# Spreading softmax reciprocals through DRAM instead of TensorE transposes, with a new order on every engine

## The chip, the cores and the metric

The kernel runs on one core of a Trainium2 chip. Its time is the device time of one execution in microseconds. Three runs of the kernel before took 716.42, 717.45 and 717.95 us; the median is 717.45 us. One further execution was profiled.

## The reference

`x` is (32, 256, 384) in float32: 32 batches of 256 nodes with 384 features. `adj` is (32, 256, 256) and is added to the attention scores. For every batch:

```python
q = x @ Wq.T;  k = x @ Wk.T;  v = x @ Wv.T + bv        # 12 heads of 32
a = einsum('bnhd,bmhd->bhnm', q, k) * 384**-0.5 + adj   # one adj for all heads
a = where(all(a == 0, axis=-1), -inf, a)
a = nan_to_num(softmax(a, axis=-1))
o = einsum('bhnm,bmhd->bnhd', a, v).reshape(B, N, 384) @ Wo.T + bo
out = layernorm(x + o)                                   # over the 384 features
```

The kernel leaves the softmax unnormalised (exponentials, and their sums per head and row), multiplies the exponentials with v, and divides the result, `o`, by the sums. The part of this case is that division. `o` stands in the bank with (head, dimension) on the partitions and the 256 rows on the free axis, while the sums stand with the rows on the partitions and (half, head) on the free axis. So the reciprocal of a sum has to be turned, and repeated over the 32 dimensions of its head, before it can be multiplied.

## The kernel before, in words

Each of the five engines runs a list of instructions of its own, and the lists meet in semaphores. The order in each list is written out by hand: `start()` for the first batches, `step(t)` for a general batch, `end()` for the last ones. There is no planner at run time: an engine that meets a wait stands still, with all that is behind it. The unit of repetition is a batch t. While TensorE is at the scores of batch t, the division and the output projection belong to batches t-1 and t-2 (`prev`, `prev2` in the code), and the first projections to t+1 and t+2 (`nxt`, `nxt2`).

What is done for a batch:

- TensorE (`block.tensor`). Every projection is done as three products of split numbers (high by high, high by low, low by high), all through line 787: `project_kq` three times (K01, Q12 into `bank_c`, K2Q0 into `bank_b`), `project_v` twice and `project_y` twice (`bank_b`). `scores` (line 836) is done for three groups of four heads. `transposes` (line 847) turns four of the twelve units of exponentials into `bank_t`; the other eight are turned by VectorE and two DMAs. `weigh` (line 877) multiplies exponentials with v, one group of four heads at a time, always into the same half of `bank_a`. `flag` (line 884) is a small product that finds out whether any row's maximum is zero. `spread` (line 858) is the step that the change removes: `spread(t, 0)` transposes `inv_wide` four times into `bank_c`, `spread(t, 1)` twice into `bank_t`.
- ScalarE. `exps` (line 559): 24 exponentials of 128x256 with their sums. `save_kq` (lines 538, 542), `copy_probT` (line 569), `save_o` (line 576, which copies the weighed bank to `o_raw`, three times), `split_o_hi` (line 584), `normalise` (line 590).
- VectorE. `add_bias` (line 1192, 24 instructions of 128x256, each with a read of its accumulator), `square` (line 1209, eight 32x32-block transposes of 128x512), `save_v` (line 1229), `find_zero` (line 1235), `read_flag` (line 1240), `mask` (a register load and a branch that is hardly ever taken into its body), `invert` (line 1264, the reciprocal of the 24 sums), `divide` (line 1273, in two parts: 128x512 out of `o_raw` and `bank_c`, 128x256 out of `o_raw` and `bank_t`), `residual` (line 1292), `moments` (lines 1297 and 1302).
- GpSimd. Splits of x, of k and q and of `o`, `permute_bias`, `add_bo`, `deviation`, and `widen_inv` (line 418), which repeats each reciprocal 32 times along the free axis for `spread`.
- SyncE issues all DMAs, in one queue (q1). `store_squares` (line 248) and `load_squares` (line 257) move a group of turned exponentials to DRAM and back, twice a batch; `load_xt`, `load_bias`, `load_xr` and `store_out` move inputs and output. SyncE too waits in its order.

The chain of the reciprocals before: `invert` (VectorE), `widen_inv` (GpSimd), `spread` (TensorE), `divide` (VectorE). The weighed bank is freed by `save_o` on ScalarE, and TensorE waits for `o_saved[g]` before it weighs the next group or runs `flag`, whose result lies in the same bank.

Of the kernel before, what the change touches and what calls it, by code (L numbers as in the profile page):

```python
# [3 lines left out]
F32 = mybir.dt.float32  # L4
# [8 lines left out]
H, HD = 12, 32  # L13
# [67 lines left out]
def build(nc, x, xT, adj, wqT, wkT, wvT, bv, woT, bo, out):  # L81
    def sb(name, shape, dt=F32):
# [23 lines left out]
    sums = [sb(f"sums{p}", [P, NT, H]) for p in range(2)]  # L106
# [15 lines left out]
    most = sb("most", [P, NT, H])  # L122
    inv = sb("inv", [P, NT, H])
    inv_wide = sb("inv_wide", [P, NT, H, HD])
    o_raw = [sb(f"o_raw{p}", [P, KC, N]) for p in range(2)]
    o_n = sb("o_n", [P, KC, N])
# [19 lines left out]
    bank = {"R0": bank_c, "K01": bank_c, "Q12": bank_c, "PV0": bank_a, "PV1": bank_a, "PV2": bank_a,  # L146
            "K2Q0": bank_b, "V0": bank_b, "V1": bank_b, "Y0": bank_b, "Y1": bank_b}
    t_flat = bank_t[:].rearrange("p k m q -> p (k m q)")
    bank["R1"] = t_flat
# [4 lines left out]
    last_bank = {"R0": s_flat[0], "Y0": s_flat[0], "R1": s_flat[1], "Y1": s_flat[1], "PV1": s_flat[2], "PV2": bank_c[:]}  # L154
# [42 lines left out]
    o_saved = [sem(f"o_saved{g}") for g in range(KC)]  # L197
# [4 lines left out]
    inv_wide_ready = sem("inv_wide_ready")  # L202
    inv_spread = sem("inv_spread")
# [11 lines left out]
    CONSTS = 4  # L215
# [7 lines left out]
    with nc.Block() as block:  # L223

        @block.sync
        def _(sp):
# [32 lines left out]

            def store_out(t):  # L260
# [27 lines left out]
            def start():  # L288
# [5 lines left out]
                load_bias(t1)  # L294
                load_xt(t2)
                load_xr(t0)
                store_squares(t0, 0)
                load_xr(t1)
                load_squares(t0, 0)
                load_xt(t3)  # L300
                store_squares(t0, 1)
                load_xt(t4)
                load_squares(t0, 1)
                load_bias(t2)
                store_squares(t1, 0)
                store_squares(t1, 1)
                load_squares(t1, 0)
                load_squares(t1, 1)
                load_bias(t3)
                store_squares(t2, 0)  # L310
                load_squares(t2, 0)
                load_xr(t2)
                store_squares(t2, 1)
                load_bias(t4)
                load_squares(t2, 1)
                store_squares(t3, 0)
                store_out(t0)

            def step(t):
                nxt2 = t.later(2)  # L320
                nxt = t.later(1)
                prev2 = t.later(-2)
                load_xt(nxt2)
                load_bias(nxt2)
                load_squares(t, 0)
                store_squares(t, 1)
                load_squares(t, 1)
                load_xr(t)
                store_squares(nxt, 0)
                store_out(prev2)  # L330

            def end():
                t28 = Batch(28)
                t29 = Batch(29)
                t30 = Batch(30)
                t31 = Batch(31)
                store_squares(t30, 1)
                load_squares(t30, 0)
                load_squares(t30, 1)
                store_squares(t31, 0)  # L340
                load_xr(t30)
                load_squares(t31, 0)
                store_squares(t31, 1)
                store_out(t28)
                load_squares(t31, 1)
                store_out(t29)
                load_xr(t31)
                store_out(t30)
                store_out(t31)

            start()
            for c in range(3, 30):
                step(Batch(c))
# [4 lines left out]
        def _(pool):  # L358
# [3 lines left out]
            pool.wait_ge(const_ready, 3)  # L362
# [41 lines left out]
            def split_o_lo(t, k):  # L404
# [5 lines left out]
                nc.gpsimd.tensor_tensor(o_lo[:, a:b], o_n[:, a:b], o_hi[:, a:b].bitcast(F32), ALU.subtract  # L410
                                        ).then_inc(o_ready, 1)
# [1143 lines left out]
```

## Time and profile before

| | |
|---|---|
| median of three runs | 717.45 us (716.42 to 717.95) |
| the profiled execution | 718.51 us |
| its span, first to last instruction | 716.2 us |
| mean granted TensorE clock | 0.997 |
| TensorE busy with matmuls | 698.7 us |
| VectorE / ScalarE / GpSimd busy | 600.1 / 613.8 / 487.2 us |
| queue q1, share of 16 DMA engines | 72.3% |

The span is 2.3 us shorter than the execution's own time; the rest lies around the first and the last instruction. A matmul's duration in the trace runs from its start to its modelled end, and the next one starts long before that end. So the time that a block of matmuls takes of TensorE is read from its start to the start of the next block. The same holds, less strongly, for VectorE and ScalarE.

### The profile page before, as it was taken

The page shows a single profiled execution, that of the slowest core. Times are in us where ns is not written, and L with a number is a line of the kernel's source. Part 1 is how long each engine was busy: PE and PEld are TensorE (multiplying, and loading weights), DVE is VectorE, ACT ScalarE, POOL GpSimd, SP SyncE. Part 2 cuts the span into 40 slices and gives each one's busy share as a digit, 9 for nine tenths or more (in the row PEclk, how much of TensorE's full clock was granted, in tenths as well). Part 3 has the DMA queues.
Part 4 walks back from the last instruction along what each step waited for, and adds up shares of the span by engine and source line. Part 5 has one row for each costly group of instructions (what it writes and reads, how often), then busy time and mean ns, then how long its engine had stood idle before and what let it go on. Part 6 is the DMA issues. An engine that isn't in the chain of part 4 may idle for free.

```text
span 716.2 us, 23143 instructions
## 1 busy us (share of the span) xinstructions
PE 698.7 (98%) x7557; PEld 600.7 (84%) x7557; DVE 600.1 (84%) x2220; ACT 613.8 (86%) x1993; POOL 487.2 (68%) x548
## 2 busy tenths in 40 slices
PE   8999999999999999999999999999999999999895
PEld 8878888888888888888888888888898888888774
DVE  4898988889888889888889888889888889888973
ACT  4889988889988889988888988889888888898882
POOL 4767666677766678766677766678766677766452
PEclk9999999999999999999999999999999999999998
DMA  8475877787777687777787777787777777777672
GB/s 266 152 278 206 300 267 264 252 315 236 263 263 273 241 309 240 265 264 267 251 302 240 262 267 259 252 305 247 257 270 261 262 291 248 255 273 259 248 288 90
DMA packets 84008, 184.61 MB, mean 258 GB/s; under 512 B 4272, under 2 KB 42928, under 8 KB 75696
## 3 DMA queue, kind: packets, MB, share of 16 engines
q1 hardware_dynamic: 83888, 183.12, 72.3%
q8 instruction: 61, 1.00, 0.6%
q14 instruction: 59, 0.48, 0.2%
HBM read 103.42 MB, written 79.69 MB: 256 GB/s over the span
## 4 chain that ended last, share of the span: by engine, by line
PE 85%; DVE 5%; DMA 4%; issue 2%; POOL 2%; ACT 1%; SPq 0%; DVEq 0%; ACTq 0%; POOLq 0%
PE bank_b L787 34%; PE bank_c L787 16%; PE bank_a L877 12%; PE s_bank L836 11%; PE bank_t L847 8%; PE bank_c L858 2%; DVE neg L1192 2%; DMA sq_dram<-w_f 2%; DMA sq_probT<-sq_dram 2%; ACT prob L559 1%; PE bank_t L858 1%; DVE w_f L1209 1%; DMA xt<-in_xT 1%; POOL kq_lo L400 0%; DVE y L1292 0%
## 5 line engine op out<-in xcount | busy, mean ns | idle before, releaser
L559 ACT ACTIVATE prob<-neg,negmax 128x256 f32<-128x256 f32 x768 | 380.3, 500 | 51.8 <-DVE w_f L1209 34.3
L1192 DVE CUSTOM_DVE_ANT_0 neg<-s_bank,bias_sq 128x256 f32<-128x256 f32 x512 | 185.2, 414 | 49.0 <-issue 42.6
L1209 DVE STREAM_TRANSPOSE w_f<-prob 128x512 f32<-128x512 f32 x256 | 173.2, 696 | 0.7 <-ACT prob L559 0.7
L559 ACT ACTIVATION_READ_ACCUMULATOR prob<-neg,negmax 128x1 f32 x768 | 147.7, 192 | 0.0
L400 POOL TENSOR_TENSOR kq_lo<-kq,kq_hi 128x512 fp32r<-128x512 f32 x96 | 125.2, 1304 | 7.7
L398 POOL CAST kq_hi<-kq 128x512 fp32r<-128x512 f32 x96 | 60.2, 627 | 79.3 <-issue 73.9
L787 PE MATMUL bank_c<-xt_hi,w_hi 128*128 128x256 f32 x384 | 111.1, 289 | 1.0 <-DVE w_lo L1171 1.0
L787 PE MATMUL bank_c<-xt_hi,w_lo 128*128 128x256 f32 x384 | 108.3, 282 | 0.0
L787 PE MATMUL bank_c<-xt_lo,w_hi 128*128 128x256 f32 x384 | 108.3, 282 | 0.0
L1192 DVE CUSTOM_DVE_ANT_0 neg<-s_bank,bias 128x256 f32<-128x256 f32 x256 | 91.0, 420 | 15.2 <-PE s_bank L836 15.0
L847 PE MATMUL bank_t<-ident,prob 128*128 128x128 f32 x512 | 80.3, 279 | 0.7 <-ACT probT L569 0.7
L569 ACT ACTIVATE probT<-bank_t 128x512 f32<-128x512 f32 x128 | 75.0, 586 | 3.6 <-PE bank_t L847 2.9
L787 PEld LDWEIGHTS bank_c<-xt_hi,w_hi 128*128 128x128 f32 x384 | 73.0, 190 | 2.1 <-issue 1.7
L410 POOL TENSOR_TENSOR o_lo<-o_n,o_hi 128x512 fp32r<-128x512 f32 (+1 forms) x62 | 63.4, 1025 | 15.4 <-ACT o_hi L584 15.4
L787 PEld LDWEIGHTS bank_c<-xt_hi,w_lo 128*128 128x128 f32 x384 | 73.1, 190 | 0.0
L787 PEld LDWEIGHTS bank_c<-xt_lo,w_hi 128*128 128x128 f32 x384 | 73.1, 190 | 0.0
L877 PE MATMUL bank_a<-sq_probT,v 128*32 128x256 f32 x1008 | 67.5, 385 | 1.2 <-DVE zero_flag L1240 1.0
L787 PE MATMUL bank_b<-w_hi,o_hi 128*128 128x384 f32 x186 | 68.3, 367 | 0.3 <-DVE y L1292 0.3
L787 PE MATMUL bank_b<-w_hi,xt_hi 128*128 128x384 f32 x192 | 67.8, 353 | 0.3 <-ACT kq L542 0.2
L836 PE MATMUL s_bank<-kq_hi 32*128 32x256 f32 x768 | 65.2, 328 | 2.6 <-POOL kq_lo L400 1.3
L836 PEld LDWEIGHTS s_bank<-kq_hi 32*128 32x128 f32 x768 | 37.3, 183 | 34.4 <-issue 33.3
L847 PEld LDWEIGHTS bank_t<-ident,prob 128*128 128x128 f32 x512 | 56.5, 140 | 10.7 <-issue 1.6
(88 smaller groups left out, 1794.1 us busy)
## 6 DMA issues: line engine op xcount, KB each, us to landing
sq_dram<-w_f SPq DMA_DIRECT2D x64, 1024.0 KB, 4.5
sq_probT<-sq_dram SPq DMA_DIRECT2D x64, 1024.0 KB, 5.6
xt<-in_xT SPq DMA_DIRECT2D x32, 384.0 KB, 4.5
xr<-in_x SPq DMA_DIRECT2D x32, 384.0 KB, 6.2
out_y<-y_out SPq DMA_DIRECT2D x31, 384.0 KB, 3.0
bias<-in_adj SPq DMA_DIRECT2D x32, 256.0 KB, 3.2
w_f<-in_wkT SPq DMA_DIRECT2D x3, 192.0 KB, 4.5
w_f<-in_wqT SPq DMA_DIRECT2D x3, 192.0 KB, 5.0
```

Of the source, the lines that this page charges most:

```text
L398: nc.gpsimd.tensor_copy(kq_hi[t.p][:, a:a + 2, :], kq[:, a:a + 2, :]).then_inc(kq_hi_ready[name], 1)
L400: nc.gpsimd.tensor_tensor(kq_lo[t.p][:, a:a + 2, :], kq[:, a:a + 2, :], kq_hi[t.p][:, a:a + 2, :].bitcast(F32), ALU.subtract).then_inc(kq_ ...
L410: nc.gpsimd.tensor_tensor(o_lo[:, a:b], o_n[:, a:b], o_hi[:, a:b].bitcast(F32), ALU.subtract).then_inc(o_ready, 1)
L559: nc.scalar.activation(prob[:, u % PROB_RING, k], neg[:, h, w.c], ACT.Exp, scale=-1.0, bias=negmax[t.p][:, w.c, h:h + 1], accum_out=sums[t ...
L569: nc.scalar.activation(probT[:, a:a + PAIR, :, P * w.c:P * (w.c + 1)], bank_t[:], ACT.Copy).then_inc(probT_act, 1)
L787: last = nc.tensor.matmul(ps, w_pair[a](k), m_pair[b](k), start=(k == 0 and e == 0), stop=(k == KC - 1 and e == 2))
L836: last = nc.tensor.matmul(s_bank[j][:, c, :], a[t.p][rows, KC + g, P * c:P * (c + 1)], b[t.p][rows, g, :], start=(e == 0), stop=(e == 2))
L847: last = nc.tensor.transpose(bank_t[:, k, m, :], prob[:, u % PROB_RING, k, P * m:P * (m + 1)], ident[:])
L858: last = nc.tensor.transpose(bank_at(t, f"R{k}")[:, at:at + P], inv_wide[:, c, JH * g:JH * (g + 1), :].rearrange("p h d -> p (h d)"), iden ...
L877: last = nc.tensor.matmul(bank_at(t, f"PV{g}")[HD * j:HD * (j + 1), 0:N], v[t.p][:, m, HD * h:HD * (h + 1)], weights, start=(m == 0), stop ...
L1192: nc.vector.tensor_tensor_reduce(out=neg[:, h, w.c], in0=s_bank[h % JH][:, w.c, :], in1=by[t.p][:, w.c, :], scale=-1.0, scalar=BIG, op0=AL ...
L1209: nc.vector.transpose(sq_stage[w.g][:, :, a:a + PAIR, :, w.c].rearrange("p b h m s -> p (h m) b s"), prob[:, u % PROB_RING].rearrange("p k ...
```

## The change

- `spread` and `widen_inv` go, and with them `inv_wide` and the banks R0 and R1. `save_o` and `o_raw` go too.
- The sums are laid out as (head in group, group, half), 24 columns. `invert` writes their reciprocals into a 128x32 tile whose last 8 columns stay at 1.0 (a new memset at the start).
- `turn_inv`, new on VectorE, waits for `invert` and transposes the 128x32 tile in 32x32 blocks.
- `store_inv`, new on SyncE, stores the turned tile to DRAM (16 KB). Four `load_inv` read it back, one for each head in group j: 768 numbers, given to 32 partitions each, into `inv_all` (128 x 3 x 256; two buffers).
- `divide` is done three times a batch, once for each group g, and reads the weighed bank itself and `inv_all`. TensorE now waits for `o_n_ready` where it waited for `o_saved`. `o_n` gets a second buffer.
- `load_xt` runs three batches ahead instead of two, `store_out` three behind instead of two, `save_kq` K01 and `project_kq` K01 two ahead instead of one.
- The order of the list of every engine is new; `step` runs over batches 3 to 28 instead of 3 to 29, and `end` covers 29 to 31.

```diff
+            def store_inv(t):
+                sp.wait_ge(inv_turned, t.count(1, 1))
+                apart(sp)
+
+                after(sp, inv_loaded[t.p], JH * (t.loads() - DMA))
+                sp.dma_start(inv_dram[t.p].rearrange("k b r -> b k r"),
+                             inv_t[:]).then_inc(inv_stored[t.p], DMA)
+
+            def load_inv(t, j):
+
+                sp.wait_ge(inv_stored[t.p], t.loads())
+                apart(sp)
+
+                after(sp, o_n_ready, t.count(KC, -KC))
+                row = inv_dram[t.p][KC * NT * j:KC * NT * (j + 1)].rearrange("k b r -> (k b r)")
+                sp.dma_start(inv_all[t.p][HD * j:HD * (j + 1)].rearrange("p g n -> p (g n)"),
+                             row.rearrange("(a n) -> a n", a=1).to_broadcast([HD, KC * N])
+                             ).then_inc(inv_loaded[t.p], DMA)
...
             def step(t):
+                nxt3 = t.later(3)
                 nxt2 = t.later(2)
                 nxt = t.later(1)
-                prev2 = t.later(-2)
-                load_xt(nxt2)
+                prev3 = t.later(-3)
                 load_bias(nxt2)
+                load_xt(nxt3)
+                store_squares(t, 1)
                 load_squares(t, 0)
-                store_squares(t, 1)
+                store_out(prev3)
+                store_inv(t)
                 load_squares(t, 1)
+                load_inv(t, 3)
+                load_inv(t, 0)
+                load_inv(t, 2)
+                load_inv(t, 1)
                 load_xr(t)
                 store_squares(nxt, 0)
-                store_out(prev2)
...
-            def widen_inv(t):
-                pool.wait_ge(inv_ready, t.count(1, 1))
-
-                after(pool, inv_spread, t.count(2))
-                apart(pool)
-                nc.gpsimd.tensor_copy(inv_wide[:], inv[:].unsqueeze(3).to_broadcast([P, NT, H, HD])
-                                      ).then_inc(inv_wide_ready, 1)
...
+            def turn_inv(t):
+                dve.wait_ge(inv_ready, t.count(1, 1))
+
+                if t.c >= 1:
+                    dve.wait_ge(inv_stored[1 - t.p], t.later(-1).loads())
+                apart(dve)
+                nc.vector.transpose(inv_t[:], inv[:]).then_inc(inv_turned, 1)
+
+            def divide(t, g):
+                dve.wait_ge(pv_done[g], t.count(1, 1))
+                if g == 0:
+                    dve.wait_ge(inv_loaded[t.p], JH * t.loads())
+
+                    after(dve, o_ready, t.count(2, -2))
+                    apart(dve)
+                nc.vector.tensor_tensor(o_n[t.p][:, g, :], bank_at(t, f"PV{g}")[:, 0:N], inv_all[t.p][:, g, :],
                                         ALU.mult).then_inc(o_n_ready, 1)
```

The new step of VectorE and of TensorE, in order:

```
VectorE: invert(t-1), turn_inv(t-1), divide(t-2,2), add_bias(t,4..7), square(t,0), save_v(t,1),
         square(t,1..3), add_bias(t,8..10), square(t,4), add_bias(t,11), divide(t-1,0), find_zero(t),
         square(t,5..7), read_flag(t), residual(t-2,0), mask(t), divide(t-1,1), add_bias(t+1,0..1),
         residual(t-2,1), add_bias(t+1,2..3), moments(t-2,0), save_v(t+1,0), moments(t-2,1)
TensorE: Q12(t+1), transposes(t-1,11), scores(t,2), weigh(t-1,0), K2Q0(t+2), K01(t+2), Y0(t-2),
         flag(t), scores(t+1,0), weigh(t-1,1), Y1(t-2), weigh(t-1,2), transposes(t,8), V0(t+1),
         scores(t+1,1), transposes(t,9), V1(t+1), transposes(t,10)
```

Here `add_bias(t,u)` stands for unit u, two instructions of 128x256. At the end, `project_y(t30, 1)` of TensorE stands ahead of `weigh(t31, 1)` instead of behind it, and SyncE's `store_inv(t31)` ahead of `load_squares(t31, 1)`.

## Rows read from the trace of the kernel before

**Rows 1.** The page, part 1: busy us, share, instructions; and one period of the windows.

```profile
PE 698.7 (98%) x7557; PEld 600.7 (84%) x7557; DVE 600.1 (84%) x2220; ACT 613.8 (86%) x1993; POOL 487.2 (68%) x548
...
306.45:327.90 21.45, 21.45 (x235) 18.47 (x234) 18.38 (x70) 18.93 (x63) 14.81 (x17) 1.00 0.77 265
```

**Rows 2.** Timeline of PE: start us, duration us, engine, line, operation, names.

```profile
301.55 0.66 PE L858 MATMUL bank_c<-ident,inv_wide 128*128 128x128 f32 x4
301.96 0.42 PE L787 MATMUL bank_b<-w_hi,o_hi 128*128 128x384 f32 x1
...
303.73 1.07 PE L877 MATMUL bank_a<-probT,v 128*32 128x256 f32 x16
304.73 0.39 PE L836 MATMUL s_bank<-kq_hi 32*128 32x256 f32 x4
...
305.63 0.66 PE L847 MATMUL bank_t<-ident,prob 128*128 128x128 f32 x4
306.05 0.42 PE L787 MATMUL bank_b<-w_hi,o_hi 128*128 128x384 f32 x1
...
307.72 0.19 PE L884 MATMUL bank_a<-zero_max,ones 128*128 128x24 bf16 x1
307.76 0.42 PE L858 MATMUL bank_t<-ident,inv_wide 128*128 128x128 f32 x2
307.93 0.36 PE L787 MATMUL bank_c<-xt_hi,w_hi 128*128 128x256 f32 x1
...
310.16 0.60 PE L847 MATMUL bank_t<-ident,prob 128*128 128x128 f32 x4
```

**Rows 3.** Groups by line of PE: line, operation, count, busy us, mean ns, idle before.

```profile
L858 PE MATMUL bank_c<-ident,inv_wide 128*128 128x128 f32 x124 | 20.1, 285 | 0.0
```

**Rows 4.** Timeline of DVE over one period, with idle time before and its releaser.

```profile
300.85 0.42 DVE L1192 CUSTOM_DVE_ANT_0 neg<-s_bank,bias 128x256 f32<-128x256 f32 x1 [0.55 <-PE s_bank L836]
...
301.20 0.42 DVE L1192 CUSTOM_DVE_ANT_0 neg<-s_bank,bias 128x256 f32<-128x256 f32 x1
...
304.50 1.29 DVE L1209 STREAM_TRANSPOSE w_f<-prob 128x512 f32<-128x512 f32 x2
305.72 0.64 DVE L1273 TENSOR_TENSOR o_n<-o_raw,bank_c 128x512 f32<-128x512 f32 x1
...
307.00 0.18 DVE L1302 BATCH_NORM_AGGREGATE meanvar<-stats 128x2 f32<-128x6 f32 x1 [0.17 <-DVE stats L1297]
...
308.39 0.41 DVE L1273 TENSOR_TENSOR o_n<-o_raw,bank_t 128x256 f32<-128x256 f32 x1
...
310.43 0.42 DVE L1192 CUSTOM_DVE_ANT_0 neg<-s_bank,bias_sq 128x256 f32<-128x256 f32 x1 [1.55 <-issue]
...
311.81 0.30 DVE L1264 RECIPROCAL inv<-sums 128x24 f32<-128x24 f32 x1
...
321.19 0.56 DVE L1229 TENSOR_TENSOR v<-bank_b,bv_all 128x384 f32<-128x384 f32 x1 [0.56 <-PE bank_b L787]
322.30 0.42 DVE L1192 CUSTOM_DVE_ANT_0 neg<-s_bank,bias 128x256 f32<-128x256 f32 x1 [0.55 <-PE s_bank L836]
```

**Rows 5.** Groups by line of ACT and of POOL for the two removed helpers.

```profile
L576 ACT ACTIVATE o_raw<-bank_a 128x256 f32<-128x256 f32 x94 | 34.8, 371 | 1.2 <-PE bank_a L877 1.1
...
L418 POOL COPY inv_wide<-inv 128x768 f32<-128x768 f32 x32 | 26.5, 829 | 3.9 <-DVE inv L1264 3.9
```

**Rows 6.** DMA issues: count, KB each, median us from issue to landing.

```profile
xr<-in_x SPq DMA_DIRECT2D x32, 384.0 KB, 6.2
out_y<-y_out SPq DMA_DIRECT2D x31, 384.0 KB, 3.0
...
bv_all<-in_bv SPq DMA_DIRECT2D x1, 192.0 KB, 7.7
```

**Rows 7.** The chain of waits in order of time, near the end: start, us, what.

```profile
693.71 5.50 DMA sq_probT<-sq_dram
```

**Rows 8.** Timeline of DVE near the end, columns as in rows 4.

```profile
695.06 0.30 DVE L1264 RECIPROCAL inv<-sums 128x24 f32<-128x24 f32 x1 [0.60 <-ACT prob L559]
```

More of the change, by code:

```diff
@@ L1000, in start @@
-                copied(t2, 10)
-                transposes(t2, 11)
-                pe.wait_ge(flag_read, t2.count(1, 1))
-                weigh(t2, 0)
             def step(t):
@@ new lines, in end @@
+                weigh(t28, 0)
+                pe.wait_ge(v_saved, t29.count(NT, 2))
+                project_y(t27, 0)
+                pe.wait_ge(o_n_ready, t28.count(KC, 1))
+                flag(t29)
+                scores(t30, 0)
+                pe.wait_ge(flag_read, t29.count(1, 1))
+                weigh(t28, 1)
+                pe.wait_ge(y_saved, t27.count(NT, 1))
+                project_y(t27, 1)
+                copied(t28, 11)
+                transposes(t29, 8)
+                pe.wait_ge(o_n_ready, t28.count(KC, 2))
@@ L1089, in end @@
-                project_y(t28, 0)
                 copied(t30, 8)
@@ new lines, in end @@
+                add_bias(t29, 9)
+                add_bias(t29, 10)
+                square(t29, 5)
+                divide(t28, 0)
+                add_bias(t29, 11)
+                find_zero(t29)
+                square(t29, 6)
+                read_flag(t29)
+                residual(t27, 0)
+                square(t29, 7)
+                mask(t29)
+                divide(t28, 1)
+                moments(t27, 0)
+                add_bias(t30, 0)
+                add_bias(t30, 1)
+                add_bias(t30, 2)
@@ L1452, in end @@
+                add_bias(t30, 3)
+                residual(t27, 1)
+                divide(t28, 2)
+                invert(t29)
+                moments(t27, 1)
+                turn_inv(t29)
+                add_bias(t30, 4)
+                add_bias(t30, 5)
+                save_v(t30, 0)
                 square(t30, 0)
-                moments(t27, 1)
+                add_bias(t30, 6)
                 square(t30, 1)
-                add_bias(t30, 4)
+                add_bias(t30, 7)
+                save_v(t30, 1)
@@ L1468, in end @@
-                square(t30, 6)
                 find_zero(t30)
-                save_v(t30, 1)
                 square(t30, 7)
                 read_flag(t30)
+                moments(t28, 0)
                 mask(t30)
+                residual(t28, 1)
+                invert(t30)
+                turn_inv(t30)
+                divide(t29, 1)
                 add_bias(t31, 0)
```

746 lines of the change are left out of this document (399 added, 347 removed).

## The prediction

> **What bounds the kernel now.** I read the page's first part, then the busy times of one period, then the timelines of TensorE and VectorE over that period. TensorE is busy in 98% of the span, and in the period from 306.45 to 327.90 it has no idle time at all, at full granted clock [rows 1]. The period is 21.45 us: VectorE's third group of scores starts at 300.85 and again at 322.30 [rows 4]. So TensorE sets the time of the middle of the kernel. VectorE is second, and nearer than its 86% says: 18.38 us busy [rows 1], 1.55 us of standing still in the flag's branch, which no other engine causes, and two waits for TensorE of 0.56 and 0.55 us [rows 4]. Take only those two away and VectorE needs 21.45 - 1.11 = 20.34 us a batch. ScalarE, with 18.93 us, and GpSimd, with 14.81, are further off [rows 1].
>
> **TensorE, the removed transposes.** What `spread` takes is read from start to start, since busy time counts overlap. The four transposes start at 301.55 and the projection behind them at 301.96: 0.41 us. The two start at 307.76 and the next block at 307.93: 0.17 us [rows 2]. Together 0.58 us a batch. By busy time the 124 would count for 20.1 us, 0.162 us each [rows 3], or 0.97 us for six; that is the most that can go. The blocks behind have a say too: the Y projection right behind a spread takes 303.73 - 301.96 = 1.77 us and the one behind other transposes 307.72 - 306.05 = 1.67 [rows 2], so 0.1 us more may go with the seam. Below, another order could make seams dearer; I know nothing that bounds this but the same differences, so 0.4 to 1.0 us, and I take 0.58, the measured start-to-start time. The new period of TensorE is 21.45 - 0.58 = 20.87 us.
>
> The Trainium skill (Perfetto Trace Analysis, Identifying the Most-Contended Engine) says that matmul busy share doesn't tell how near TensorE is to its limit and asks for the share of weight loading. By that measure TensorE stands at 84% [rows 1], level with VectorE's 84% and ScalarE's 86%, and the removal would buy little; the gapless period speaks for TensorE all the same, and I keep its number.
>
> **ScalarE and GpSimd.** Three copies of 0.371 us and one of 0.829 us a batch go [rows 5]: 1.11 and 0.83 us. Neither engine ended a wait of the steady period, so I cost both at nothing. What they give is slack: ScalarE then needs about 17.8 us of 20.87.
>
> **VectorE.** Before, the two divisions take 0.64 and 0.41 us; three of 0.41 are 1.23, so +0.18 at most (their operands are of the same two kinds, bank and SBUF). `turn_inv` is a block transpose of 128x32; the nearest row is that of two 128x512, 1.29 us in all, hence 0.65 for one and, by columns alone, 0.04; I take 0.15 (bounds 0.04 and 0.65). It stands right behind `invert` and waits for its end: 0.17 us as between the two steps of the moments [rows 4]. Sum: +0.50 us. On the other side, `residual` now stands between `read_flag` and the branch. The sequencer can take the flag's load and the branch while the 128x384 addition runs, which like `save_v`'s lasts 0.56 us [rows 4], so the 1.55 us can shrink by 0 to 0.56; I take 0.4. VectorE's need: 20.34 + 0.50 - 0.40 = 20.44 us, and 20.84 if nothing shrinks. Both lie under 20.87, but the second by 0.03 only.
>
> **Does the bank come free in time?** ScalarE's prompt copy is replaced by a division in VectorE's strict order, and TensorE now waits for it before `flag`, `weigh(t-1,1)` and `weigh(t-1,2)`. Queued behind `flag` is everything: the next batch's scores too. I laid the two lists beside each other. `flag_read` is ready one division, a `find_zero`, three squares (1.9 us) and a reduction after VectorE comes to `divide(t-1,0)`: about 2.8 us. TensorE asks for it only after `flag` and one group of scores (305.63 - 304.73 = 0.90 us [rows 2]). So TensorE must come to `flag` 1.9 us or more after VectorE comes to the division. The limit from the other side is V0(t+1), which VectorE wants for `save_v` about 8.8 us after that division (the instructions between, by the durations above and below). On TensorE it ends a group of scores 0.9, two weighings of 1.0 (303.73 to 304.73), two projections of 1.7 and a transposition of 0.42 [rows 2] behind `flag`: 6.7 us. So TensorE may come to `flag` at most 2.1 us after VectorE comes to the division: the window in which neither waits is some 0.2 us wide. A miss of 0.1 or 0.2 us a batch is likely, and a part of it falls on VectorE, which has slack. I take 0.03 us a batch on TensorE as the cost: period 20.90.
>
> **SyncE and the new round trip.** SyncE issues five more DMAs a batch. None of its waits ends on a steady-state wait of TensorE now. `load_squares(t,1)` goes behind `store_inv(t)`, hence behind `invert(t)`; it is then issued about 12 us before its weighing, which is enough with 6 us of landing. The chain that matters runs from `turn_inv(t-1)` to `divide(t-1,0)`. In VectorE's order there lie a division (0.41), four units at 0.70 (two instructions 0.35 apart: 300.85 to 301.20), a square 0.61, `save_v` 0.56, three squares 1.83, three units 2.1, a square 0.61 and a unit 0.70 [rows 4]: 9.6 us. The chain needs an issue (0.1), a landing of the 16 KB, three further issues at 0.4 before the last load is out, and its landing. The nearest row for a small undisturbed transfer is the output's, 3.0 us; for a load that stands in the queue behind a load of squares, as here, it is `xr`'s, 6.2 us; the one broadcast to many partitions is `bv_all`, 7.7 us at the crowded start [rows 6]. Low: 0.1 + 3.0 + 1.2 + 3.0 = 7.3. High: 0.1 + 6.2 + 1.2 + 7.7 = 15.2. I take 0.1 + 2.5 + 1.2 + 5 = 8.8 us, since the four loads are 384 KB together and the queue before `store_inv` has been empty for some microseconds: it fits, with 0.8 us to spare. The new bytes are 0.4 MB on some 5.9 MB a batch, so the 0.77 share of the DMA engines [rows 1] goes to about 0.85 in the shorter period.
>
> A rule speaks against this step. The Trainium skill (DMA: Bandwidth & Descriptors, Why a DMA increments its semaphore by 16 and not by 1) says that a DMA is spread over the largest number up to 16 that divides the slowest dimension of both sides. The store's DRAM side has a slowest dimension of 4, so by it four engines would carry 32 pieces of 128 bytes each, which lengthens the landing. No row here shows such a store; it speaks for the second rival below.
>
> **Start and end.** The first 42 us are set by loading and filling and keep their length. The steady gain holds from there to about 674 us: 632/21.45 = 29.5 periods. In the last batch the load of the second squares, issued at 693.71 with 5.50 us to land [rows 7], now goes behind `store_inv(t31)`, and the reciprocal starts at 695.06 [rows 8]: with 0.3 + 0.17 + 0.15 and two issues it goes out at about 696.2, 2.5 us later. Then the inverse loads land behind it, about 1 us more, before three divisions. Against this, `project_y(t30, 1)` (1.7 us) no longer stands behind the last squares' weighing, `widen_inv` and the last `spread` are gone. I take +0.7 us for the end (bounds 0 and +3).
>
> **The sum.** -0.55 x 29.5 = -16.2; +0.7; together -15.5 us. From the profiled execution: 718.5 - 15.5 = 703.0. The median of the runs shown lies 1.06 us under that execution, so 702.
>
> **The rivals.**
>
> 1. VectorE becomes the bound. For it: 20.84 us without any shrinking of the branch, and the narrow window. Against it: the residual in front of the branch. With a period of 21.2 us the gain is 0.25 x 29.5 = 7.4, less 0.7: 711. Chance 0.17.
>
> 2. The reciprocals come late, and the kernel is slower. Place: VectorE stands before `divide(t-1,0)` for the fourth load; TensorE then stands before `flag`. It decides once the chain exceeds 9.6 us, and turns the sign at 9.6 + 0.55 = about 10.1. Price: with 0.1 + 3.0 + 1.2 + 6.2 = 10.5, and one more 0.6 for pieces of 128 bytes or a queue that has grown, 11.1 us: 1.5 us late, a period of 22.4 less what slack hides, say 22.0. +0.55 x 29.5 = +16, +0.7: 734. For it: `xr`'s 6.2 us, behind the same kind of load. Against it: those 6.2 us count the wait behind a full load of squares from its issue, and here most of that runs while the store is landing. Chance 0.13. Falling short only by 0.6 us or so gives the same time as before; 0.03.
>
> 3. The seams shrink as well. Near the upper bound of 1.0 above, the period comes to 20.5 us: -0.95 x 29.5 = -28, +0.7: 690. For it: the Y block's 0.1 us. Against it: VectorE needs 20.44 at best. Chance 0.15.
>
> 4. The change doesn't do what it says, that is, the transposes were hidden in other work and their removal gives nothing. Against it stands the gapless TensorE. It is in rival 2's last chance.
>
> **How the numbers follow.** Forecast 0.52 (697 to 708), rival 1 0.17, rival 3 0.15, no change 0.03, slower 0.13. Within 0.2%, or 1.4 us, is what a measurement can't tell from no change. Faster 0.52 + 0.17 + 0.15 = 0.84, same 0.03, slower 0.13. The range has to leave out the slower case, 0.13, and little else: 689 to 716 leaves out about 0.19 with the far end of rival 3.
>
> **What would show it.** Right: the period between two starts of VectorE's third group of scores is 20.8 to 21.0 us, TensorE stays gapless in it, no steady wait of VectorE names the DMA of `inv_all`. The gap before the instruction behind the branch is 1.0 to 1.2 us; if it is 1.55, rival 1 gains. Rival 2 would show as idle time of line `divide` released by the DMA `inv_all<-inv_dram`, and as TensorE idle before `flag`. Rival 3 would show as Y and V blocks of 1.67 us and less throughout. The last squares' load lands about 2.5 us later against the last reciprocal than before. Wrong is the forecast if TensorE's own idle time in a period is over 0.3 us, or if its blocks don't add up to 20.9.

## The result and the profile after

The changed kernel takes 713.56 us (712.95 to 713.71, four runs) against 717.68 us (716.42 to 717.95): ratio 0.9935, 95% interval 0.9918 to 0.9952. It is faster, by 4.1 us and not by the 15 to 16 forecast; 702 was the prediction and 716 the upper end of its range. The sign and the binding engine were right; the size of the gain was wrong by a factor of more than three. Medians and ranges in this document are over executions in the chip's fast state; only the run with the loads first in every batch had slow ones, four of ten.

The page of the changed kernel, lines of parts 1 and 2, then one of the DMA issues (part 6), to lay beside [rows 1, 6]:

```profile
PE 686.2 (96%) x7362; PEld 585.9 (82%) x7362; DVE 619.7 (87%) x2284; ACT 585.2 (82%) x1897; POOL 462.9 (65%) x517
...
PE   8999999999999999999999999999999999989784
...
PEclk9999999999999999999999999999999999999997
...
inv_all<-inv_dram SPq DMA_DIRECT2D x128, 96.0 KB, 4.6
```

The last slices of the PE line are thin; so I cut the span by the instruction that reads the flag (`read_flag`, line 1240 before, 1298 after), which stands once in each batch:

| from, to | before, us | after, us | difference |
|---|---|---|---|
| start to flag 3 | 94.4 | 90.9 | -3.5 |
| flag 3 to flag 28 (25 periods) | 536.1 (21.444 each) | 525.7 (21.027 each) | -10.4 |
| flag 28 to flag 29 | 21.45 | 22.30 | +0.85 |
| flag 29 to flag 30 | 18.42 | 22.01 | +3.6 |
| flag 30 to flag 31 | 23.07 | 20.59 | -2.5 |
| flag 31 to the last instruction, SyncE's included | 20.8 | 27.7 | +7.0 |

Up to the flag of batch 28 the changed kernel is 13.9 us ahead in these two traces, and 8.9 of them are given back in the last three and a half batches. The 3.5 us of the start are not settled: the eleven traces with the start of the changed kernel (its own and those of the experiments below, bar the run without the trip and the one in the old order) reach flag 3 between 90.9 and 94.0 us, and the 90.9 here is at the low end.

One period of the changed kernel, from the windows (columns: PE, PEld, DVE, ACT, POOL busy, clock, DMA share, GB/s):

```profile
301.20:322.23 21.03, 21.03 (x235) 18.00 (x232) 19.15 (x73) 18.05 (x60) 14.54 (x17) 1.00 0.89 291
```

TensorE is as gapless as in [rows 1]; VectorE is busy for 0.77 us more, ScalarE for 0.88 less. The timeline of VectorE in the same period:

```profile
302.71 0.42 DVE L1345 TENSOR_TENSOR o_n<-bank_a,inv_all 128x256 f32<-128x256 f32 x1 [0.92 <-PE bank_a L931]
...
308.95 0.30 DVE L1327 RECIPROCAL inv<-sums 128x24 f32<-128x24 f32 x1
309.43 0.21 DVE L1336 STREAM_TRANSPOSE inv_t<-inv 128x32 f32<-128x32 f32 x1 [0.18 <-DVE inv L1327]
```

Where the branch stood before with 1.55 us of idle time [rows 4], the gap is 0.92 us and ends with a weighing of TensorE, so VectorE is not what the period waits for.

Most of VectorE's extra time is neither the turn nor the divisions. `find_zero`, one small operation of 128x24, takes 1.12 us in the mean of the 25 periods where it took 0.47 before, though it has the same size and types. VectorE's and GpSimd's timelines side by side show what it waits for; the same period:

```profile
319.31 1.19 DVE L1293 TENSOR_SCALAR zero_max<-negmax 128x24 bf16<-128x24 f32 x1
```

```profile
319.17 1.29 POOL L470 TENSOR_TENSOR kq_lo<-kq,kq_hi 128x512 fp32r<-128x512 f32 x1
```

`find_zero` ends at 320.50, 0.04 us after GpSimd's operation at 320.46. Where GpSimd does nothing at that moment, as for batches 30 and 31, `find_zero` takes 0.18 us. The new orders put it at the start of a GpSimd operation; in the old order it came near the end of one. In the middle this costs nothing, since TensorE is gapless all the same. At the end it does, as is seen below.

The round trip comes next, from SyncE's timeline: the store goes out at 309.73 and the first of the four loads at 311.71, as soon as it has landed. The last of the four has landed 8.6 us after the start of the turn at the latest, and the division starts 9.55 us after it.

```profile
309.73 0.51 SPq L268 DMA_DIRECT2D inv_dram<-inv_t  x1
310.35 0.41 SPq L260 DMA_DIRECT2D sq_probT<-sq_dram  x1
311.71 1.72 SPq L278 DMA_DIRECT2D inv_all<-inv_dram  x4
```

In the middle nobody waits for these loads for long (VectorE stands before a division four times without a releaser in the profile, 1.1 us in all). For batch 28, the last before `end`, somebody does. VectorE's, GpSimd's and TensorE's timelines:

```profile
635.60 0.42 DVE L1345 TENSOR_TENSOR o_n<-bank_a,inv_all 128x256 f32<-128x256 f32 x1 [1.32 <-DMA inv_all<-inv_dram]
...
636.74 1.62 DVE L1293 TENSOR_SCALAR zero_max<-negmax 128x24 bf16<-128x24 f32 x1
```

```profile
636.52 1.81 POOL L498 TENSOR_TENSOR xr<-xr,bo_all 128x768 f32<-128x768 f32 x1 [2.61 <-DMA xr<-in_x]
```

```profile
638.50 0.17 PE L938 MATMUL bank_a<-zero_max,ones 128*128 128x24 bf16 x1 [2.63 <-DVE zero_max L1293]
...
639.95 1.51 PE L931 MATMUL bank_a<-sq_probT,v 128*32 128x256 f32 x12
```

The flag product waits for `find_zero`, which stands behind the division, which waits for the loads. The loads are the smaller half of it. Late by 1.32 us, VectorE comes to `find_zero` 0.22 us after GpSimd has begun to add `bo` to `xr`, and `find_zero` takes 1.62 us instead of 0.18: it ends 0.03 us after that addition. So TensorE stands for 2.63 us. Then the clock falls: the window from that flag to the next has a mean of 0.92, where all the middle has 1.00. By windows of 2 us the granted clock is 0.74 from 638, 0.50 from 640 and 0.90 from 642, and 1.00 again from 644, so part of it ran at 1.2 GHz; the 12 of 16 matmuls in the last row take 1.51 us, where before all 16 took 1.07 [rows 2].

```profile
638.90:660.91 22.01, 21.03 (x213) 16.82 (x208) 19.37 (x75) 17.64 (x58) 7.00 (x9) 0.92 0.81 259
```

### The profile page after: what moved, and what is told of

It reads as the page before. It is cut to its first block, busy times and chain, and to the rows that moved or that the text cites. A ratio compares the mean times of both kernels' runs of the same rounds, so it can differ in the third digit from the quotient of the medians.

```text
span 711.3 us, 22854 instructions
## 1 busy us (share of the span) xinstructions
PE 686.2 (96%) x7362; PEld 585.9 (82%) x7362; DVE 619.7 (87%) x2284; ACT 585.2 (82%) x1897; POOL 462.9 (65%) x517
## 4 chain that ended last, share of the span: by engine, by line
PE 88%; DVE 4%; DMA 3%; issue 2%; POOL 2%; SPq 1%; ACT 1%; DVEq 0%; ACTq 0%; POOLq 0%
PE bank_b L853 37%; PE bank_c L853 18%; PE bank_a L931 13%; PE s_bank L902 11%; PE bank_t L913 8%; DMA inv_all<-inv_dram 2%; DVE neg L1250 1%; DMA inv_dram<-inv_t 1%; DMA xt<-in_xT 1%; PE s_bank L853 1%; DVE w_f L1267 1%; POOL xt_lo L459 0%; POOL kq_lo L470 0%; ACT prob L625 0%; SPq L278 0%
## 5 line engine op out<-in xcount | busy, mean ns | idle before, releaser
L1250 DVE CUSTOM_DVE_ANT_0 neg<-s_bank,bias_sq 128x256 f32<-128x256 f32 x512 | 183.3, 419 | 6.8 <-PE s_bank L902 4.3
L1267 DVE STREAM_TRANSPOSE w_f<-prob 128x512 f32<-128x512 f32 x256 | 169.8, 690 | 1.3 <-ACT prob L625 0.4
L625 ACT ACTIVATION_READ_ACCUMULATOR prob<-neg,negmax 128x1 f32 x768 | 150.1, 195 | 0.0
L488 POOL TENSOR_SCALAR var_eps<-meanvar 128x2 f32<-128x2 f32 x32 | 7.3, 227 | 119.0 <-DVE meanvar L1373 119.0
L853 PE MATMUL bank_b<-w_hi,xt_hi 128*128 128x384 f32 x192 | 70.2, 366 | 1.6 <-DVE v L1287 1.6
```

Source lines behind the costliest of these rows:

```text
L488: nc.gpsimd.tensor_scalar(var_eps[:], meanvar[:, :, 1], EPS, None, ALU.add).then_inc(var_ready, 1)
L625: nc.scalar.activation(prob[:, u % PROB_RING, k], neg[:, h, w.c], ACT.Exp, scale=-1.0, bias=negmax[t.p][:, w.c, h:h + 1], accum_out=sums[t ...
L853: last = nc.tensor.matmul(ps, w_pair[a](k), m_pair[b](k), start=(k == 0 and e == 0), stop=(k == KC - 1 and e == 2))
L1250: nc.vector.tensor_tensor_reduce(out=neg[:, h, w.c], in0=s_bank[h % JH][:, w.c, :], in1=by[t.p][:, w.c, :], scale=-1.0, scalar=BIG, op0=AL ...
L1267: nc.vector.transpose(sq_stage[w.g][:, :, a:a + PAIR, :, w.c].rearrange("p b h m s -> p (h m) b s"), prob[:, u % PROB_RING].rearrange("p k ...
```

## The experiments

Periods are means over the 25 from flag 3 to flag 28 of each run's trace, the stretches are from flag to flag. The traces are the better measure here: the total times of one kernel scattered by 1 to 8 us in these runs, and where the step is that of the changed kernel the mean period is 21.03 in every trace.

**Is it the round trip or the new end?** The trip taken out altogether; VectorE multiplies by a tile of ones:

```diff
 def store_inv(t):
-    sp.wait_ge(inv_turned, ...); ...; sp.dma_start(inv_dram...)
+    return
 def load_inv(t, j):
-    sp.wait_ge(inv_stored[t.p], t.loads()); ...; sp.dma_start(inv_all...)
+    return
 def divide(t, g):
-        dve.wait_ge(inv_loaded[t.p], JH * t.loads())
```

> The changed kernel without the round trip: no store and no loads of the reciprocals, VectorE multiplies by a tile of ones (the division is left out). In the changed kernel the steady period is 21.03 us and the stretch from the flag reduction of batch 28 to the end is 94.7 us, against 85.7 us before the change. Theory A (the end is long because the reciprocals come late: VectorE waits 1.3 us for batch 28's and 1.0 us for batch 31's, TensorE then 2.6 us before the flag product, and its clock falls): the stretch shrinks to 89 us or less, total 713.5 - 6 = 707.5 or less; steady period still 21.03. Theory B (the new hand-made end order itself is worse, whatever the reciprocals do): the stretch stays at 93 us or more, total 712 or more. Theory C (the seven per cent more DMA traffic also lengthens the middle): the period falls under 21.0.

Measured: 707.9 us (0.9872 of the kernel before, 0.9844 to 0.9900); period 21.027; flags 28 to 31: 19.69, 20.46, 20.45; from flag 28 to the last engine instruction 85.2 instead of 92.6 us. Theory A: 7.5 of the 8.9 us hang on the round trip, directly or through what it sets off. The period doesn't move with 7% less traffic (theory C falls). The other 1.5 us are what is left over; I put them down to the end's order, and no run shows that.

**Only batch 28's wait taken away:**

```diff
-                    dve.wait_ge(inv_loaded[t.p], JH * t.loads())
+                    if t.c == 28:
+                        dve.wait_ge(inv_loaded[1], JH * t.later(-1).loads())
+                    else:
+                        dve.wait_ge(inv_loaded[t.p], JH * t.loads())
...
-    inv_all[t.p][:, g, :]
+    inv_all[1 if t.c == 28 else t.p][:, g, :]
```

> As the changed kernel, but batch 28 is divided by batch 27's reciprocals, which are there long before (so batch 28's output is not the reference's). Theory A in its narrow form (one late round trip, that of batch 28, starts the loss): the flag-to-flag time from 28 to 29 falls from 22.3 to about 21, TensorE's 2.6 us of idle time before the flag product of batch 29 goes with the lowered clock behind it, and the total falls by 3 to 5 us to about 709 to 710. Theory B: the gap moves to the next wait and the total falls by less than 1.5 us.

Measured: 710.4 us (709.1 to 711.9), flags 28 to 31: 19.46, 20.51, 20.78, that is 60.75 instead of 64.90 us. One wait of 1.32 us on VectorE costs 4.15 us in the end: 2.84 from flag 28 to 29, 1.50 from 29 to 30 with the lower clock, and 0.19 come back after it. The clock is at full in that stretch now, and there is no idle time before the flag product. `find_zero` is done before GpSimd begins, at 638.39:

```profile
636.82 0.18 DVE L1293 TENSOR_SCALAR zero_max<-negmax 128x24 bf16<-128x24 f32 x1
```

So the 2.84 us are about half the loads (`find_zero` starts 1.44 us later, measured from the flag) and half the longer `find_zero` (1.44 us).

**The general step for batch 29 too:**

```diff
-            for c in range(3, 29):
+            for c in range(3, 30):
                 step(Batch(c))
             end()                  # less what step(29) has done, on every engine
```

> The changed kernel with the general step also for batch 29; the rest of the end keeps its order, less what the step has done. Theory B (the end's order for batch 29 is short of filling between weigh(28,0) and the flag product: one K projection instead of two): the times from flag 28 to 29 becomes 21.0 instead of 22.3, and 29 to 30 falls from 22.0 to 20 or less, total 709 to 711. Theory A: the round trip of batch 28 is as late as in every other step, where VectorE has no wait for it, so here too it goes away; the two agree on this run, and e2 tells them apart. If the total is not under 712.5, the loss lies behind batch 30.

Measured: 711.85 us (711.0 to 715.1); flags 28 to 31: 21.03, 21.54, 21.64. In the step's order batch 28's reciprocals are in time for two reasons: they have landed 9.1 us after the turn at the latest, where the end's order has them at 10.0, and VectorE asks after 9.56 us instead of 8.82. The rest of the end, written for another state of the engines, gives most of it back: flag 29 to 30 is 21.5, not the 20 expected. Against the kernel before the total is 0.9941 (0.9918 to 0.9965), no better than that of the change.

**More small products before the last projections:**

```diff
-                keep_warm(23)
+                keep_warm(60)
```

> The changed kernel with 60 instead of 23 small products ahead of the last two output projections. In the changed kernel these run with a first matmul form of 474 ns mean, against 352 ns before the change, after 2.3 us of idle time. If the lowered clock costs there, the 18 matmuls take 3.4 instead of 5.0 us and the total falls by about 1.6 us to 712. If the products end late, or the chain behind is bound by another engine, 713.5 or more.

Measured: the last 18 matmuls take 3.43 instead of 4.98 us, as expected, and flag 31 to the end 26.1 instead of 27.7. In the changed kernel the 23 products end 2.3 us before `o_lo` is ready. GpSimd has a part in that too: VectorE's two splits into `o_lo` take 1.87 us while GpSimd's last addition to `xr` runs, and 1.03 in the run without the trip, where it comes later. The total, 714.2 (711.2 to 714.7), doesn't show it; the scatter is larger than the effect.

**The spreading alone, in the old order:**

```diff
 def spread(t, k):        # TensorE
-    ...
+    return
 def widen_inv(t):        # GpSimd
-    ...
+    return
```

> The kernel before with nothing but the spreading taken out: no widen_inv on GpSimd, no spread on TensorE, VectorE multiplies by ones (the division is left out); all orders as before. It measures the term of the sum by itself. If the six transposes are worth their start-to-start time, the period falls from 21.45 by 0.58 to 20.87 us. If they are worth their busy time, by 1.0 to 20.5. If it comes to 0.42, as the whole change gave, the new orders' seams cost nothing. VectorE's own need was worked out as 20.34 us, so it should not be the bound at 20.87. Total 717.5 - 0.58 x 30 = about 700.

VectorE multiplies by ones here too. Measured: 716.9 us, ratio 0.9988 (0.9972 to 1.0005): no change. The periods scatter from 20.83 to 22.10, mean 21.35. TensorE now waits, in its list of waits:

```profile
PE s_bank L833 <- DVE negmax L1181: 8.3, 23, 0.6
PE bank_a L873 <- DVE zero_max L1224: 2.8, 4, 1.0
```

So my expectation of 20.87 was wrong: in the old order TensorE has hardly come forward when it meets VectorE, whose `add_bias` it waits for 23 times. What I had called VectorE's spare time there could not be used. I take it that the 1.55 us of the branch stand in the way, which no run shows. The transposes' time was had with the new orders, and not without them.

**Are seams bought by a swap of neighbours?**

```diff
                 project_v(nxt, 0)
-                scores(nxt, 1)
 
                 copied(t, 8)
                 transposes(t, 9)
+                scores(nxt, 1)
```

> The changed kernel with two neighbours of TensorE's step swapped: transposes(t,9) now stands right behind V0(t+1), and scores(t+1,1) behind it. In the trace of the changed kernel a projection followed by a transposition or a projection gives way 0.17 us after its last matmul starts, one followed by scores or a weighing 0.27 us. Theory (seams are a cost of TensorE and the middle is bound by it alone): the period falls from 21.03 by 0.1 to 20.93 us, total -2.5 us, 711. Rival (VectorE or ScalarE is at its limit too): unchanged at 21.03, or longer since ScalarE waits for the bank of the transpositions.

Measured: period 21.04, unchanged (716.7 us, 711.8 to 720.0). The projection in front now gives way after 1.68 instead of 1.77 us, but the transposition that stands before the scores takes 0.53 instead of 0.42. The price moved with the scores: it belongs to the switch into them, not to what stands before. That made the next theory. The total is above the changed kernel's though the period is the same: this trace is 3.0 us later at flag 3, and its `find_zero` of batch 29 lasted 1.66 us, with TensorE idle for 3.2 and the clock at 0.88 in the next stretch.

**One more switch:**

```diff
                 scores(t, 2)
 
-                pe.wait_ge(o_n_ready, prev2.count(KC, 3))
-                weigh(prev, 0)
-
                 pe.wait_ge(v_saved, t.count(NT, 2))
                 project_kq(nxt2, "K2Q0")
 
+                pe.wait_ge(o_n_ready, prev2.count(KC, 3))
+                weigh(prev, 0)
```

> The changed kernel with weigh(t-1,0) moved behind K2Q0(t+2) in TensorE's step, so that scores(t,2) and weigh(t-1,0) no longer stand together. Theory (what the new order loses on TensorE is one more switch from full-width products to the row- or column-tiled ones of scores and weighings: three runs of them a period before the change, four after, each 0.1 us on the way in and 0.08 on the way out): a fifth run makes the period 21.03 + 0.16 to 0.19 = 21.2 us, total +4 to 5 us, 718. Rival (no such price; the 0.16 us went elsewhere): 21.03 us, total unchanged at 713.5.

Measured: period 21.194, +0.167, with TensorE as gapless as before (718.6 us, 715.1 to 722.7):

```profile
303.04:324.23 21.19, 21.19 (x230) 18.02 (x228) 19.17 (x72) 18.02 (x60) 14.53 (x17) 1.00 0.88 292
```

The expectation of 0.16 to 0.19 us is met: each run of scores and weighings costs that much beside its matmuls, and the change had made four runs out of three.

**The queue in front of the loads:**

```diff
                 store_inv(t)
-                load_squares(t, 1)
                 load_inv(t, 3)
                 load_inv(t, 0)
                 load_inv(t, 2)
                 load_inv(t, 1)
+                load_squares(t, 1)
```

> The changed kernel with the four loads of the reciprocals ahead of load_squares(t,1) in the general step and in batch 29 (batches 30 and 31 as they are). Theory (the late arrival for batch 28 is queueing behind that load of 1 MB): the reciprocals of batch 28 land 3 us earlier, VectorE doesn't wait for them, flag 28 to 29 is 19.5 us, and the total falls by 3 to 4 us to 710, as in the run in which batch 28 did not wait. Rival (they are late because they are issued late): less than 1 us earlier. The period stays 21.03, since the squares have several microseconds to spare before their weighing; if not, weigh(t-1,1) waits and the period grows.

The same was done for batch 29 in the end. Measured: flag 28 to 29 is 19.47 us, so batch 28 is cured. But the mean period grows to 21.264; single ones reach 22.8, and TensorE waits for the squares:

```profile
PE bank_a L931 <- DMA sq_probT<-sq_dram: 5.4, 6, 1.7
```

Total 717.7 us (711.4 to 718.5), ratio 0.9968 (0.9939 to 0.9997). The squares had no "several microseconds" either. The Trainium skill (DMA: Bandwidth & Descriptors, Queues, rings and completion order) says that descriptors of a queue are consumed in ring order on each DMA engine; that what goes first decides who is late, on both sides, agrees with it.

**How much room has the trip in the middle?**

```diff
                 load_squares(t, 1)
+                load_xr(t)
                 load_inv(t, 3)
...
-                load_xr(t)
```

> The changed kernel with load_xr(t), 384 KB, ahead of the four loads of the reciprocals in the general step: it delays them by some 1 to 1.5 us and asks how much room the round trip has in the middle. If the room is under that, VectorE waits in line of divide for the DMA in every step and the period grows from 21.03 by what is missing, 0.3 to 1 us (total 721 to 738). If it is 2 us or more, the period is unchanged and only batch 28 is later by 1 to 1.5 us: total 714 to 716.

Measured: mean period 21.158; most periods are 21.03, two are 22.8 with one of 20.8 behind each, and TensorE waits 0.7 us for `find_zero` and 0.7 for the flag where that happens. The room is about 1 us, and in those steps the transfer of 384 KB takes more. Total 715.45 us (712.4 to 720.4).

Batch 28 came out with 20.95 us, against expectation, though its loads were 1.45 us late for VectorE, more than in the changed kernel. `find_zero` is the difference. GpSimd's addition began early enough, at 639.77, to be over when VectorE came:

```profile
641.69 0.18 DVE L1293 TENSOR_SCALAR zero_max<-negmax 128x24 bf16<-128x24 f32 x1
```

```profile
642.01 0.17 PE L938 MATMUL bank_a<-zero_max,ones 128*128 128x24 bf16 x1 [1.31 <-DVE zero_max L1293]
```

TensorE stood for 1.31 us instead of 2.63, the clock stayed at 1.00 and the next stretch took 20.45 us. So late loads alone cost this kernel 1.5 us (20.95 against 19.46 without the wait), and the other 2.7 of the 4.15 come with the GpSimd operation in `find_zero`'s way. This is a comparison of traces; no run moved that operation alone.

**Both findings put together: the loads first, for batch 28 alone.**

```diff
-                load_squares(t, 1)
+                if t.c != 28:
+                    load_squares(t, 1)
                 load_inv(t, 3)
...
                 load_inv(t, 1)
+                if t.c == 28:
+                    load_squares(t, 1)
```

> The changed kernel with the four loads of the reciprocals ahead of load_squares(t,1) for batch 28 alone. Both earlier findings together: the period stays 21.03 (it grew to 21.26 when the loads went first in every batch, since the squares then came late), and flag 28 to 29 is 19.5 us as with them first or without any wait. Total 713.5 - 3 to 4 = about 710. If the squares of batch 28 come late for their weighing, flag 29 to 30 grows from 20.5 and the total is 712 or more.

Measured: 709.48 us (708.65 to 712.24), 0.9875 of the kernel before (0.9848 to 0.9901); period 21.027; flags 28 to 31: 19.47, 20.75, 20.33. VectorE reaches the division at 636.52 and doesn't wait, with the last load out some 4.7 us before:

```profile
628.08 0.52 SPq L268 DMA_DIRECT2D inv_dram<-inv_t  x1
630.08 2.06 SPq L278 DMA_DIRECT2D inv_all<-inv_dram  x4
```

It beats both kernels: the change itself is at 0.9935 (0.9918 to 0.9952).

**The very end as well, twice** (on top of the run before):

```diff
-                store_out(t28)
                 store_inv(t31)
...
                 load_inv(t31, 3)
+                store_out(t28)
...
+                invert(t31)
+                turn_inv(t31)
                 divide(t30, 1)
-                invert(t31)
-                turn_inv(t31)
...
-                keep_warm(23)
+                keep_warm(60)
```

> As the run before it, and at the very end: 60 small products instead of 23, invert(31) and turn_inv(31) ahead of divide(30,1), store_out(28) behind the loads of batch 31's reciprocals instead of ahead of their store. Theory: the last reciprocals are stored about 1 us earlier and land 1 to 2 us earlier than the 12 us after their turn of the changed kernel, and the last 18 output matmuls take 3.4 instead of 5.0 us: total 2 to 3 us under the run before, 707 to 708, faster than both kernels. Rival (the last squares' weighing, not the reciprocals, is what the end waits for): only the clock's 1.6 us, 708.5 to 709; or, if the small products run past the moment at which the last split is ready, nothing.

Measured: 714.9 us (713.0 to 717.1), worse than the run before it. Two things went wrong. The later `store_out` kept the single output buffer full, which ScalarE's waits show, and TensorE's wait for the `residual` behind it was 4.9 us:

```profile
ACT y_out L653 <- DMA out_y<-y_out: 6.1, 1, 6.1
```

And in this execution the clock was low for some microseconds, in the stretch where TensorE has little to do (flag 30 to 31 took 23.42 instead of 20.33 us):

```profile
662.00:672.00 10.00, 7.29 (x48) 6.04 (x49) 8.90 (x37) 9.40 (x33) 4.54 (x7) 0.66 1.00 303
```

The second time `store_out(t28)` stayed where the change had put it, and the rest of the diff was kept.

> The run in which batch 28's reciprocals go first (709.5 us), with 60 small products instead of 23 before the last output projections, and invert(31) with turn_inv(31) ahead of divide(30,1); store_out(28) stays where the change put it, since behind the loads it kept ScalarE waiting 6.1 us for the one output buffer and TensorE 4.9 us. Theory: the last 18 matmuls take 3.4 instead of 5.0 us, the store of the last reciprocals goes out about 1 us earlier; from the flag of batch 31 to the end 25 to 26 us instead of 27.6, total about 708. Rival: the few microseconds are lost again in TensorE's clock, which falls in some executions in the thin stretch of batch 31's scores (0.66 granted over 10 us in the last run, flag 30 to 31 23.4 instead of 20.3 us): 710 to 712.

Measured: 710.7 us (707.8 to 712.6), 0.9886 (0.9858 to 0.9914). Flag 31 to the end is 26.1 us, as expected, but flag 30 to 31 was 21.1 instead of 20.3, and the median is not below that of the run with batch 28 alone. Between the two versions nothing is shown; both are faster than the changed kernel. The clock had a part in it: that stretch was at a mean of 0.92 in this trace and at 1.00 in the other.

## Why the prediction was wrong

**TensorE's removed transposes, right with a term missing.** The 0.58 us are real, but the net is 0.42 us a period. I read the seams one by one and took "another order could make seams dearer" as unknown. It could have been counted from the two orders: before, TensorE goes from full-width products into scores or weighings three times a period (scores(t,2) with weigh(t-1,1); weigh(t-1,2) with scores(t+1,0); weigh(t,0) with scores(t+1,1)), after it four times, since weigh(t-1,2) and scores(t+1,1) stand alone. One run costs 0.167 us (the split run), and 0.58 - 0.167 = 0.41. So the term was mis-sized by a price for the order that I put at nothing; the 0.03 us beside it stood for the narrow window of the bank. Over 25 periods that is 3.3 of the missing microseconds.

**VectorE, mostly right.** `turn_inv` takes 0.21 us where I had 0.15, behind a wait of 0.18 where I had 0.17. The gap of the branch fell from 1.55 to at most 0.92 us, by more than the bound of 0.56. What the sum lacked is `find_zero`, 0.65 us longer in the mean because GpSimd is at work as it starts. I took the durations of single operations from the old order, and this one is not its own. I forecast that VectorE would not bind, and it doesn't in the new order. But my 20.34 us for its need in the old order led to a wrong expectation for the spreading taken out alone: a sum of durations and waits is not the whole need where the order fixes when each instruction may begin.

**The bank freed in time: right in the middle.** TensorE has no idle time there at all. The window of 0.2 us was missed all the same, on the side with slack: VectorE waits 0.42 us for V0 and 0.92 for a weighing in a period. **The round trip in the middle: right**, at most 8.6 us against 8.8 forecast, and room of about 1 us where 0.8 was forecast. The store in pieces of 128 bytes, which spoke for rival 2, let its reader go after 1.98 us, less than the 2.5 I took. Rival 2 named the mechanism and its place (VectorE before `divide(t-1,0)`, TensorE before `flag`), but as a thing of every step, where it would have made the kernel slower.

**The end: this is the step that failed.** It said +0.7 us, with bounds 0 and +3. The stretch from flag 28 on was to take the steady gain for about two batches too, -1.1, so -0.4 in all, and came out 8.9 us longer. I had looked there at the last batch alone. The rival's mechanism struck once, at batch 28, where the new end order brings VectorE to the division 0.7 us sooner and has TensorE ask for the flag behind one K projection, not two. By the run without that wait it costs 4.15 us, by the run with the loads first 4.35. The price is so much above the 1.32 us of lateness for two things that the rival did not have: GpSimd's addition holds up `find_zero`, and the clock falls behind TensorE's longer stand. From flag 31 on the run without any trip gains another 3.2 us (24.6 against 27.7). By the two traces 1.5 of them are the clock in the last projections, 1.0 the way from the last division through the splits to the last projections, and 0.6 the last divisions themselves. The 1.5 us left over are without a run of their own. These add to 8.9: 4.15 + 3.2 + 1.5. The start, where I had forecast nothing but the first 42 us unchanged, gave 3.5 us by flag 3 in this pair of traces, 2 us more than its share of periods; by the scatter of 90.9 to 94.0 that is no finding.

**The numbers.** With -3.5 at the start, -10.4 in the middle and +8.9 at the end the sum is -5.0; the spans, 716.2 and 711.3 us, differ by 4.9. Against the forecast of -15.5 the end is worse by 9.3 and the middle by 3.3, and the start is better by 2.2. That the result lies between 689 and 716 is luck: the upper part of the range was there for rival 1, whose 711 is near the result, but VectorE doesn't bind, and no rival had the end as its place.

## What to carry to other kernels

Where lists are ordered by hand, cost the first and the last batches with the same care as the step: walk each wait of the new path through them, and give every transfer that has a microsecond of room in the step a look where the order changes. A transfer that is just in time has two neighbours in its queue, and putting it first makes another late; do it in the one place that needs it. Look at what GpSimd does when a small VectorE operation starts on which TensorE waits, since the small one may last as long as the large one beside it. Count the switches between kinds of products when blocks change places, not only the blocks.

## What the runs showed of the hardware

- `find_zero`, a VectorE operation on 128x24 values (float32 to bfloat16, all in SBUF), takes 0.18 us with GpSimd idle. Where a GpSimd operation is under way as it starts, it lasts until that one has ended: 1.19 us beside `kq_lo` in most periods, 1.62 beside `xr` at batch 29. Over the fourteen traces it ran 34 times beside nothing, for 0.17 or 0.18 us, and 414 times into a GpSimd operation; in 412 of these it ended 0.02 to 0.06 us after that operation, and in the other two, with 0.11 us or less of it left, it took its 0.17 or 0.18.
- A run of row-tiled or column-tiled matmuls between full-width ones costs 0.167 us a time in this step: the period went from 21.027 to 21.194 us with one more, and stayed (21.04) when only the neighbour before the scores changed from a projection to a transposition.
- A 128x32 block transpose on VectorE takes 0.21 us, a 128x512 one 0.71. The store of 16 KB in pieces of 128 bytes let its first reader be issued 1.98 us after it in the middle of the kernel. For batch 31 it was 4.2 us in the changed kernel (684.26 to 688.49) and anything from 2.0 to 4.8 in the other traces of the new orders; why is open.
- After 2.63 us of idle time and scores alone, TensorE's granted clock fell to the lower of its levels for part of the next stretch (mean 0.92, and 0.50 from 640 to 642 us); after 1.31 us of idle time at the same place it did not. From flag 30 to 31, where the matmuls of the changed end keep TensorE busy for 15 us at full clock, the mean clock was 1.00 in five traces (20.3 to 20.8 us), 0.92 in five (21.1 to 21.6) and 0.78 in two (23.4 and 23.5), which is part of the scatter of the total times. The last 18 output matmuls took 4.98 us after 2.3 us of idle time, and 3.43 us with small products in it.
